# Fast form of the last convolution: even, odd and difference products of half width for every sample

## The chip, the cores and the metric

The kernel runs on one core of one Trainium2 chip. The metric is the device time of one execution in microseconds; the median of three runs of the kernel before is 755.43 us (754.4 to 756.1).

## The reference, cut to what matters

```python
def _layer(x, style, w, b, mw, mb, typ):
    s = style @ mw.T + mb                       # modulation, one vector per sample
    weight = SCALE * w * s[:, None, :, None]
    demod = lax.rsqrt(jnp.sum(weight * weight, axis=(2, 3)) + EPS)
    weight = weight * demod[:, :, None, None]
    if typ == 'same':         out = vmap(_conv_same)(x, weight) + b[None, :, None]
    elif typ == 'upsample':   out = _blur(vmap(_conv_up)(x, ...) + b[None, :, None], 2.0 * blur_k, (1, 1))
    elif typ == 'downsample': out = vmap(_conv_down)(_blur(x, blur_k, (2, 2)), weight) + b[None, :, None]
    return out
out = x
for i, typ in enumerate(('same', 'upsample', 'same', 'downsample')):
    out = _layer(out, style, weights[i], biases[i], mod_w[i], mod_b[i], typ)
return x + out                                  # x: (128, 64, 1024) float32
```

Each sample goes through four short convolutions whose weights are its own. Nothing nonlinear lies between them, so for one sample the four layers and the added x are one linear convolution (apart from two columns at each end, which are computed separately).

## The kernel before, in words

The samples are taken in 32 **groups** of four (g is the group, i the sample in it, b = 4g + i), and in 64 pairs (n) for loads, splits and stores.

For each sample the kernel first **composes** the four layers into one filter of five taps, 128 x 128 each: inputs and outputs hold even positions in partitions 0 to 63 and odd ones in 64 to 127, so a sample is 128 x 512 and the filter steps over columns. Composing is done for a whole group at once in seven **units** (g, u): u 0 and 1 make `Q2f`, u 2 and 3 make `Gf`, u 4, 5 and 6 make the taps `Wf`. A unit is 2 to 14 matmuls of 256 columns into one of four PSUM banks `pg`; then VectorE (`full`) scales the bank into `Q2f`, `Gf` or `Wf`, ScalarE (`high`) rounds it to a high part, and GpSimd (`low`, POOL in the profile) or, for the taps, VectorE (`w_low`) subtracts to get the low part. A group has 56 matmuls in its units: 10 in u 0 and 1, 24 in u 2 and 3, 22 in u 4 to 6. The lower and upper halves of the taps' other columns are filled by DMAs within SBUF (`cross`, on SP's queue).

The **convolution** of a sample (`conv`) is 5 taps x 3 products (high x high, high x low, low x high; `split_mm`) of 512 columns into `po[b % 2]`: 15 matmuls. Its x is loaded (`load`), rounded on ScalarE (`x_high`, 128 x 1032 for a pair) and its remainder taken on VectorE (`x_low`). ScalarE's `t_out` scales `po`, adds the bias term and writes `T`; GpSimd's `finish` copies the four end columns from `EP` into `T`; SP stores the pair (`store`). The end columns of 32 samples at a time come from `edge`, four steps of small matmuls on TensorE and chains of small operations on VectorE.

The order is written by hand. `SLOTS` says which units stand ahead of which sample: units 4 to 6 of the next group at i = 0, units 0 and 1 of the group after that at i = 1, unit 2 at i = 2 and unit 3 at i = 3. Every engine runs its own list in order and waits on semaphores.

## Time and profile before

| | |
|---|---|
| median of 3 runs | 755.43 us (754.4 to 756.1) |
| span of the profiled execution, first to last instruction | 755.1 us |
| TensorE busy | 711.5 us (94%), 3858 matmuls |
| VectorE, ScalarE, GpSimd busy | 342.5, 299.5, 281.6 us |
| mean granted TensorE clock | 0.982 of 2.4 GHz |

Matmul records overlap, since matmuls are pipelined: what one costs is read as the distance between the starts of two that follow one another. A row's own duration runs to the modelled end of its last column. For the other engines, durations are those of single instructions, and the next one starts some 0.09 us before the record of the one ahead of it ends. Idle time ahead of an instruction is in brackets, with what ended it.

### The profile page before, as it was taken

The numbers are of one execution on the slowest core, as the hardware profiler recorded it, in microseconds if no ns is written. First come the engines' busy times: TensorE is split into PE (matmuls) and PEld (weight loads), VectorE is DVE, ScalarE is ACT, GpSimd is POOL, SyncE is SP. The second block draws the span as 40 slices with busy tenths as digits, with TensorE's granted clock in tenths as the row PEclk, the third lists the DMA queues.
The fourth block names the chain that finished last, engine by engine and source line by source line (L and its number), as shares of the span: only waits on it lengthen the run. The fifth ranks groups of instructions, "written<-read, shape, count | busy, mean of one in ns | idle before, by whom it ended". The sixth has DMA issues, their size and how long they took to land.

```text
span 755.1 us, 10500 instructions
## 1 busy us (share of the span) xinstructions
PE 711.5 (94%) x3858; PEld 622.0 (82%) x3858; DVE 342.5 (45%) x551; ACT 299.5 (40%) x437; POOL 281.6 (37%) x456
## 2 busy tenths in 40 slices
PE   5668999998999999998999999999899999999997
PEld 4557888887888888887888888888788888888886
DVE  5968434435544333445335443453454443334430
ACT  3322444343434344434243444443334444443432
POOL 2431443442333443333443434434334434443310
PEclk9979999999999999999999999999999999999999
DMA  7043267764367767655756666677445777666572
GB/s 253 1 118 64 84 147 175 175 147 118 99 162 175 157 145 166 154 138 115 175 120 155 151 152 148 150 175 175 107 108 137 174 175 170 148 150 164 157 177 83
DMA packets 112162, 108.46 MB, mean 144 GB/s; under 512 B 4528, under 2 KB 78640, under 8 KB 112112
## 3 DMA queue, kind: packets, MB, share of 16 engines
q1 hardware_dynamic: 111456, 106.22, 58.6%
q10 hardware_dynamic: 656, 1.57, 0.6%
q8 instruction: 31, 0.51, 0.3%
q14 instruction: 19, 0.16, 0.1%
HBM read 36.47 MB, written 33.55 MB: 93 GB/s over the span
## 4 chain that ended last, share of the span: by engine, by line
PE 77%; DVE 10%; issue 6%; POOL 3%; ACT 2%; DMA 1%; POOLq 0%; ACTq 0%; DVEq 0%
PE po L159 16%; PE po L161 16%; PE po L160 16%; PE pg L159 7%; PE pg L161 6%; PE pg L160 6%; PE pg L164 3%; PE pg L165 3%; POOL Q2l L520 2%; DVE xl L595 1%; DVE Wf L617 1%; DVE Q2f L606 1%; POOL Q2h L168 1%; ACT Q2h L418 1%; ACT W L428 1%
## 5 line engine op out<-in xcount | busy, mean ns | idle before, releaser
L159 PE MATMUL po<-xh,W 128*128 128x512 f32 x640 | 254.5, 398 | 0.0
L160 PE MATMUL po<-xl,W 128*128 128x512 f32 x640 | 253.4, 396 | 0.0
L161 PE MATMUL po<-xh,W 128*128 128x512 f32 x640 | 253.4, 396 | 0.0
L595 DVE TENSOR_TENSOR xl<-X,xh 128x1032 fp32r<-128x1032 f32 x64 | 81.8, 1277 | 201.3 <-ACT xh L396 201.1
L403 ACT ACTIVATE T<-po,cv,DD 128x512 f32<-128x512 f32 x128 | 99.7, 779 | 169.2 <-PE po L161 167.7
L161 PEld LDWEIGHTS po<-xh,W 128*128 128x128 f32 x640 | 125.2, 196 | 24.5
L159 PEld LDWEIGHTS po<-xh,W 128*128 128x128 f32 x640 | 125.8, 197 | 20.6 <-issue 0.2
L160 PEld LDWEIGHTS po<-xl,W 128*128 128x128 f32 x640 | 125.6, 196 | 20.1
L520 POOL TENSOR_TENSOR Q2l<-Q2f,Q2h 128x512 fp32r<-128x512 f32 x31 | 40.0, 1290 | 228.3 <-ACT Q2h L418 228.3
L428 ACT CAST W<-Wf 128x512 fp32r<-128x512 f32 x64 | 46.6, 728 | 119.3 <-DVE Wf L617 93.0
L613 DVE TENSOR_TENSOR Gf<-pg,D10c 128x512 f32<-128x512 f32 x64 | 44.0, 689 | 103.8 <-PE pg L165 103.6
L528 POOL TENSOR_TENSOR Gl<-Gf,Gh 128x512 fp32r<-128x512 f32 x31 | 40.0, 1291 | 121.1 <-ACT Gh L423 121.1
L423 ACT CAST Gh<-Gf 128x512 fp32r<-128x512 f32 x64 | 39.6, 620 | 113.6 <-DVE Gf L613 113.6
L159 PE MATMUL pg<-Q2h,B1h 128*128 128x256 f32 x192 | 59.2, 309 | 19.6 <-POOL Q2h L168 15.7
L396 ACT CAST xh<-X 128x1032 fp32r<-128x1032 f32 x64 | 66.7, 1042 | 0.0
L159 PEld LDWEIGHTS pg<-Q2h,B1h 128*128 128x128 f32 x192 | 38.7, 202 | 33.2 <-issue 28.9
L159 PE MATMUL pg<-Gh,Ch 128*128 128x256 f32 x192 | 56.8, 296 | 1.3 <-DVE Gl L754 1.3
L630 DVE TENSOR_TENSOR W<-Wf,W 128x512 fp32r<-128x512 f32 x64 | 52.3, 817 | 11.0 <-ACT W L428 11.0
L161 PE MATMUL pg<-Q2h,B1l 128*128 128x256 f32 x192 | 56.9, 296 | 0.0
L160 PE MATMUL pg<-Q2l,B1h 128*128 128x256 f32 x192 | 56.8, 296 | 0.0
L160 PE MATMUL pg<-Gl,Ch 128*128 128x256 f32 x192 | 54.8, 285 | 0.0
L161 PE MATMUL pg<-Gh,Cl 128*128 128x256 f32 x192 | 54.8, 285 | 0.0
(154 smaller groups left out, 998.2 us busy)
## 6 DMA issues: line engine op xcount, KB each, us to landing
X<-in_xin SPq DMA_DIRECT2D x64, 516.0 KB, 5.3
out<-T SPq DMA_DIRECT2D x64, 512.0 KB, 3.1
W<-W SPq DMA_DIRECT2D x96, 256.0 KB, 6.6
W<-W SPq DMA_DIRECT2D x32, 384.0 KB, 7.6
E<-in_ed ACTq DMA_DIRECT2D x1, 768.0 KB, 8.5
XE<-in_xe SPq DMA_DIRECT2D x1, 576.0 KB, 11.1
Gf<-in_mwt SPq DMA_DIRECT2D x1, 256.0 KB, 3.2
A2f<-in_a ACTq DMA_DIRECT2D x1, 256.0 KB, 6.3
```

Source lines behind the costliest of these rows:

```text
L159: eng.matmul(o, wh_, rh, start=first, stop=False)
L160: eng.matmul(o, wh_, rl, start=False, stop=False)
L161: return eng.matmul(o, wl_, rh, start=False, stop=last)
L396: act.copy(xh[:, n % XH], X[:, n % XR]).then_inc(s_xh, 1)
L403: act.activation(T[:, n % TR, b % Q], po[b % 2][:, :], ACT.Identity, bias=cv[:, b:b + 1], scale=DD[:, 3, b:b + 1]).then_inc(s_t, 1)
L423: act.copy(Gh[:, :, v], Gf[:, :, v]).then_inc(s_gh, 1)
L428: act.copy(W[:, g % 2, v, 0, :, 0].rearrange("p v a m -> p a v m"), Wf[:, :, v]).then_inc(s_wh, 1)
L520: pool.tensor_tensor(Q2l[:], Q2f[:, :, 0:2], r32(Q2h[:, :, 0:2]), ALU.subtract).then_inc(s_q2l, 1)
L528: pool.tensor_tensor(Gl[:, :, 0:2], Gf[:, :, 0:2], r32(Gh[:, :, 0:2]), ALU.subtract).then_inc(s_gl, 1)
L595: tt(xl[:, n % XH], X[:, n % XR], r32(xh[:, n % XH]), ALU.subtract).then_inc(s_xl, 1)
L613: m = tt(cols(Gf[:, :, 2 * u - 4:2 * u - 2]), cols(bank(src, 2)), bc2(gs(D10c, g), 2), ALU.mult)
L630: tt(w[1], Wf[:, :, v], r32(w[0]), ALU.subtract).then_inc(s_wl, 1)
```

## The change

**The convolution in three products.** A sample is now held as 2 x 256 columns (even columns, odd columns, `H = 256`) and a third set, their difference (odd minus the next even, `columns(n)` on GpSimd). With the taps W0 to W4, `conv_even` multiplies the even columns by W0, W2, W4 into `pa` (which lies in the bank `ps`), `conv_odd` the odd ones by W1, W3 into `pb[b % 2]`, and `conv_diff` the differences by C1 = W0 - W1, C3 = W2 - W3 and W4 on top of `pb`. Each tap is 3 matmuls of 256 columns: 24 per sample in place of 15 of 512. W, xh, xl and X grow by the new taps and columns.

**The results.** ScalarE's `t_out` becomes `a_out` (pa, scaled and with bias, into `AB`) and `b_out` (pb, scaled, into `AB`). The even columns are their sum, taken on GpSimd (`even_out`); the odd ones are `pb` after `conv_diff`, scaled, plus the shifted first part, on VectorE (`odd_out`). `conv_diff(b - 1)` stands between `conv_even(b)` and `conv_odd(b)`, and waits until `b_out(b - 1)` has read `pb`.

**The taps.** VectorE makes the differences (`w_diff`, two per group); ScalarE rounds and VectorE subtracts in three parts in place of two, `w_high` and `w_low` (3 taps, 4 taps, and two taps of 64 partitions in `M`). `cross` has six DMAs in place of four, 1664 KB per group in place of 1152 KB.

**Other.** `finish` is gone: the end columns go out once, in an output of their own (`oute`), and are put in place on the host. The edge steps stand at i = 3 of every second group on TensorE and at i = 2 of the group after it on VectorE; before, those of the first 32 samples all stood in group 0. X has 3 buffers in place of 4, xh and xl 2 in place of 3, T 2 in place of 3. Units move: none at i = 1; 2 and 3 together at i = 2; 0 and 1, now of the group three ahead, at i = 3; and units 2 and 3 of group 1 are composed before the first sample. In the diff, the last three loops over b are those of ScalarE, GpSimd and VectorE.

```diff
-PROLOGUE = [(0, 0), (0, 1), (0, 2), (0, 3), (1, 0), (1, 1), (0, 4), (0, 5), (0, 6)]
...
-SLOTS = [[(1, 4), (1, 5), (1, 6)], [(2, 0), (2, 1)], [(2, 2)], [(2, 3)]]
+PROLOGUE = [(0, 0), (0, 1), (0, 2), (0, 3), (1, 0), (1, 1), (0, 4), (0, 5), (0, 6), (1, 2), (1, 3)]
...
+SLOTS = [[(1, 4), (1, 5), (1, 6)], [], [(2, 2), (2, 3)], [(3, 0), (3, 1)]]
...
+            def taps(b, o, e, js, onto=False):
+                g, i = divmod(b, NG)
+                n, q = divmod(b, Q)
+                for k, (j, start, stop) in enumerate(js):
+                    w = [W[:, g % 2, j - C1, t, i // 2].rearrange("p r (o b) -> p (r o) b", b=2)[:, :, i % 2]
+                         for t in range(2)]
+                    m = split_mm(pe, o, w[0], w[1], xh[:, n % XH, q, e, k:k + H], xl[:, n % XH, q, e, k:k + H], start, stop, onto)
+                return m
...
+            def conv_even(b):
                 g, i = divmod(b, NG)
                 n, q = divmod(b, Q)
                 if i == 0:
-                    pe.wait_ge(s_wh, 2 * g + 2)
-                    pe.wait_ge(s_wl, 2 * g + 2)
-                    pe.wait_ge(s_w[g % 2], 2 * 16 * ND * (g // 2 + 1))
+                    pe.wait_ge(s_wh, 3 * g + 2)
+                    pe.wait_ge(s_wl, 3 * g + 2)
+                    pe.wait_ge(s_w[g % 2], 16 * NX * (g // 2 + 1))
                 if q == 0:
                     pe.wait_ge(s_xh, n + 1)
                     pe.wait_ge(s_xl, n + 1)
+                if b:
+                    pe.wait_ge(s_ae, b)
+                taps(b, pa, 0, ((W0, True, False), (W2, False, False), (W4, False, True))).then_inc(s_a, 1)
+
+            def conv_odd(b):
                 if b >= 2:
-                    pe.wait_ge(s_t, b - 1)
-                for j in range(5):
-                    w = [W[:, g % 2, j, t, i // 2].rearrange("p r (o b) -> p (r o) b", b=2)[:, :, i % 2] for t in range(2)]
-                    m = split_mm(pe, po[b % 2][:, :], w[0], w[1], xh[:, n % XH, q, j:j + L2], xl[:, n % XH, q, j:j + L2],
-                                 j == 0, j == 4)
-                m.then_inc(s_o, 1)
+                    pe.wait_ge(s_yo, b - 1)
+                taps(b, pb[b % 2][:, 0:H], 1, ((W1, True, False), (W3, False, True))).then_inc(s_b, 1)
+
+            def conv_diff(b):
+                pe.wait_ge(s_be, b + 1)
+                taps(b, pb[b % 2][:, 0:H], 2, ((C1, False, False), (C3, False, False), (W4, False, True)),
+                     True).then_inc(s_p, 1)
...
             for b in range(B):
+                g, i = divmod(b, NG)
                 for x in units_of(b):
                     unit(*x)
-                conv(b)
-                if divmod(b, NG) in edge_at:
-                    edge(*edge_at[divmod(b, NG)])
+                conv_even(b)
+                if b:
+                    conv_diff(b - 1)
+                conv_odd(b)
+                if i == 3 and g % 2 == 0:
+                    edge(*divmod(g // 2, 4))
...
             def x_high(n):
                 act.wait_ge(s_x[n % XR], 16 * (n // XR + 1))
+                act.wait_ge(s_s, n + 1)
                 if n >= XH:
-                    act.wait_ge(s_o, Q * (n - XH + 1))
+                    act.wait_ge(s_p, Q * (n - XH + 1))
                 act.copy(xh[:, n % XH], X[:, n % XR]).then_inc(s_xh, 1)
...
                 g, i = divmod(b, NG)
-                if b == 1:
+                if b:
+                    b_out(b - 1)
+                else:
                     act.wait_ge(s_sc, SC_CV)
-                if b:
-                    t_out(b - 1)
-                if b % Q == 0 and b // Q + 2 < NQ:
-                    x_high(b // Q + 2)
+                n = (b + 1) // Q
+                if b % Q == 1 and XH <= n < NQ:
+                    x_high(n)
+                if i == 1 and g + 3 < NGR:
+                    q3_high(g + 3)
+                if i == 0:
+                    a_out(b)
                 for x in units_of(b):
-                    if x[1] != 5:
+                    if x[1] == 4:
+                        for k in range(3):
+                            w_high(x[0], k)
+                    elif x[1] < 4:
                         high(*x)
-                if i == 3 and g + 3 < NGR:
-                    q3_high(g + 3)
-            t_out(B - 1)
+                if i:
+                    a_out(b)
...
+                if b:
+                    even_out(b - 1)
+                n = b // Q + 1
+                if b % Q == 0 and XH <= n < NQ:
+                    columns(n)
+                if i == 0 and g + 3 < NGR:
+                    q3_full(g + 3)
                 for x in units_of(b):
                     if x[1] < 4:
                         low(*x)
-                if i == 2 and g + 3 < NGR:
-                    q3_full(g + 3)
-                if i == 3 and g + 3 < NGR:
+                if i == 1 and g + 3 < NGR:
                     q3_low(g + 3)
-                if b % Q == 1 and b > Q:
-                    finish(b // Q - 1)
-            finish(NQ - 1)
+                if i == 3 and g + 2 < NGR:
+                    identity(g + 2)
...
-                    c, k = edge_at[g, i]
+                    if x[1] == 4:
+                        w_diff(x[0], 0)
+                    elif x[1] == 6:
+                        w_diff(x[0], 1)
+                if b:
+                    odd_out(b - 1)
+                n = (b + 1) // Q
+                if b % Q == 1 and XH <= n < NQ:
+                    x_low(n)
+                for x in units_of(b):
+                    if x[1] == 4:
+                        for k in range(3):
+                            w_low(x[0], k)
+                if i == 2 and g % 2 == 1:
+                    c, k = divmod(g // 2, 4)
                     edge(c, k)
```

On ScalarE, at i = 0 of a group (`AB<-ps` is a_out, `AB<-pb` is b_out, `M` holds the two taps of 64 partitions), before:

```order
L428 CAST W<-Wf 128x2x2x128
L428 CAST W<-Wf 128x2x3x128
L403 ACTIVATE T<-po0,cv,DD 128x512
L418 CAST Q2h<-Q2f 128x2x256
L418 CAST Q2h<-Q2f 128x2x128
```

and of the change, from i = 0 to a_out of i = 1:

```order
L447 ACTIVATE AB<-pb1,DD 128x256 [waits b]
L442 ACTIVATE AB<-ps,cv,DD 128x256 [waits yo,ye,a]
L473 CAST W<-Wf 128x2x3x128 [waits p,cd]
L473 CAST W<-Wf 128x2x4x128 [waits p,cd]
L477 CAST M<-Wf 64x2x2x128 [waits w1,cd]
L447 ACTIVATE AB<-pb0,DD 128x256 [waits b]
L435 CAST xh<-X 128x1548 [waits p,s,x0]
L453 CAST Q3h<-Q3f 128x512 [waits c,q3f]
L442 ACTIVATE AB<-ps,cv,DD 128x256 [waits yo,ye,a]
```

The three roundings of the taps now stand between a_out of sample 0 and b_out of sample 0. On GpSimd, the same stretch (from the low parts of units 0 and 1 at i = 3 on), before:

```order
L520 TENSOR_TENSOR Q2l<-Q2f,Q2h 128x512 [waits q2h]
L168 TENSOR_TENSOR Q2h<-Q2f,Q2h 64x2x128 [waits q2l,q2h]
L546 COPY T<-EP 128x2x2 [waits ed,t,q2l]
L547 COPY T<-EP 128x2x2
L528 TENSOR_TENSOR Gl<-Gf,Gh 128x2x256 [waits gh]
```

and of the change:

```order
L582 TENSOR_TENSOR Q2l<-Q2f,Q2h 128x512 [waits q2h]
L180 TENSOR_TENSOR Q2h<-Q2f,Q2h 64x2x128 [waits q2l,q2h]
L601 TENSOR_TENSOR ID<-EYE,inv3 128x256 [waits ce,q2l]
L618 TENSOR_TENSOR T<-AB 128x256 [waits be,ae]
L609 TENSOR_TENSOR X<-X 128x2x257 [waits x2]
L569 TENSOR_TENSOR Q3f<-q3s,D32 128x256 [waits q3l,q3h]
L569 TENSOR_TENSOR Q3f<-q3s,D32 128x256
L618 TENSOR_TENSOR T<-AB 128x256 [waits st0,be,ae]
```

even_out (`T<-AB`) and the difference columns (`X<-X`) have come in between. On VectorE, from x_low at i = 3 to the low parts of the taps at i = 0, of the change:

```order
L674 TENSOR_TENSOR xl<-X,xh 128x1548 [waits xh]
L698 TENSOR_TENSOR Wf<-pg,S 128x2x256 [waits wh,c]
L708 TENSOR_TENSOR Wf<-Wf 128x2x256 [waits ce]
L698 TENSOR_TENSOR Wf<-pg,S 128x2x256 [waits wh,c]
L702 TENSOR_TENSOR Wf<-Wf,ID 64x2x128 [waits id,ch]
L698 TENSOR_TENSOR Wf<-pg,S 128x2x128 [waits wh,c]
L711 TENSOR_TENSOR Wf<-Wf 128x2x2x128 [waits ce]
L729 SCALAR_TENSOR_TENSOR T<-pb,DD,AB 128x256 [waits p,ae]
L716 TENSOR_TENSOR W<-Wf,W 128x2x3x128 [waits wh]
L716 TENSOR_TENSOR W<-Wf,W 128x2x4x128 [waits wh]
L720 TENSOR_TENSOR M<-Wf,M 64x2x2x128 [waits w1,wh]
```

Before, the same stretch there was x_low, the three `Wf<-pg` with the `Wf<-Wf,ID` between them, and two low parts; the two differences (`Wf<-Wf` alone), odd_out (`T<-pb,DD,AB`) and the low part in `M` are new.

## Rows read from the trace of the kernel before

**Rows 1.** Timeline, TensorE: start us, duration us, engine, line, operation, tiles, shape.

```profile
432.50 0.40 PE L161 MATMUL po<-xh,W 128*128 128x512 f32 x1
432.73 0.27 PE L159 MATMUL pg<-Q2h,B1h 128*128 128x256 f32 x1
432.84 0.28 PE L160 MATMUL pg<-Q2l,B1h 128*128 128x256 f32 x1
```

**Rows 2.** Timeline, TensorE: the same place of two groups of samples, one after the other.

```profile
427.50 0.36 PE L159 MATMUL pg<-Q2h,B1h 128*128 128x256 f32 x1
...
448.44 0.36 PE L159 MATMUL pg<-Q2h,B1h 128*128 128x256 f32 x1
```

**Rows 3.** Timeline, TensorE with its weight loads (PEld), from composing to a sample.

```profile
308.62 0.19 PEld L165 LDWEIGHTS pg<-Q3h,A2l 128*128 128x128 f32 x1
...
308.74 0.20 PEld L159 LDWEIGHTS po<-xh,W 128*128 128x128 f32 x1
...
308.86 0.40 PE L159 MATMUL po<-xh,W 128*128 128x512 f32 x1
```

**Rows 4.** Groups of instructions by shape: count | busy us, mean ns | idle before, releaser.

```profile
L403 ACT ACTIVATE T<-po,cv,DD 128x512 f32<-128x512 f32 x128 | 99.7, 779 | 169.2 <-PE po L161 167.7
...
L396 ACT CAST xh<-X 128x1032 fp32r<-128x1032 f32 x64 | 66.7, 1042 | 0.0
L159 PE MATMUL pg<-Q2h,B1h 128*128 128x256 f32 x192 | 59.2, 309 | 19.6 <-POOL Q2h L168 15.7 <-DVE Q2h L168 3.0
...
L520 POOL TENSOR_TENSOR Q2l<-Q2f,Q2h 128x512 fp32r<-128x512 f32 x31 | 40.0, 1290 | 228.3 <-ACT Q2h L418 228.3
...
L630 DVE TENSOR_TENSOR W<-Wf,W 128x768 fp32r<-128x768 f32 x32 | 30.7, 959 | 10.3 <-ACT W L428 10.3
L428 ACT CAST W<-Wf 128x768 fp32r<-128x768 f32 x32 | 26.7, 835 | 26.3 <-DVE Wf L623 26.3
...
L512 POOL TENSOR_TENSOR Q3l<-Q3f,Q3h 128x256 fp32r<-128x256 f32 x31 | 23.2, 750 | 6.3 <-ACT Q3h L410 4.1
...
L539 POOL TENSOR_TENSOR ID<-EYE,inv 128x256 f32<-128x256 f32 x32 | 20.0, 624 | 7.6 <-DVE inv L760 7.6
...
L608 DVE TENSOR_TENSOR Q2f<-pg,D 128x256 f32<-128x256 f32 x32 | 13.3, 415 | 0.0
```

**Rows 5.** Timeline, GpSimd (POOL) beside VectorE (DVE), before the first sample.

```profile
37.54 1.65 POOL L507 TENSOR_TENSOR Q3f<-q3s,D 128x256 f32<-128x256 f32 x2
38.02 0.69 DVE L630 TENSOR_TENSOR W<-Wf,W 128x512 fp32r<-128x512 f32 x1 [0.68 <-ACT W L428]
...
41.87 1.23 DVE L595 TENSOR_TENSOR xl<-X,xh 128x1032 fp32r<-128x1032 f32 x1
...
42.52 1.17 POOL L512 TENSOR_TENSOR Q3l<-Q3f,Q3h 128x256 fp32r<-128x256 f32 x1 [3.33 <-ACT Q3h L410]
```

**Rows 6.** Timeline, the same two engines later, in the main loop.

```profile
180.16 1.35 DVE L595 TENSOR_TENSOR xl<-X,xh 128x1032 fp32r<-128x1032 f32 x1 [2.28 <-ACT xh L396]
180.48 1.07 POOL L546 COPY T<-EP 128x4 f32<-128x4 f32 x1
...
181.50 0.18 POOL L547 COPY T<-EP 128x4 f32<-128x4 f32 x1
```

**Rows 7.** Stretch with taps in flight: busy us of each engine, clock, DMA share, GB/s.

```profile
318.00:323.00 5.00, 5.00 (x28) 4.42 (x27) 0.69 (x1) 2.24 (x4) 3.52 (x6) 1.00 1.23 196
```

**Rows 8.** Timeline: edge step 0 on TensorE, edge step 1 on VectorE (first and last row).

```profile
53.76 1.30 PE L326 MATMUL pe<-b1s,E 128*128 128x224 f32 x6
...
62.32 0.39 DVE L646 TENSOR_TENSOR AA<-pe,S 128x224 f32<-128x224 f32 x1 [1.49 <-PE pe L330]
...
65.98 1.05 DVE L658 SCALAR_TENSOR_TENSOR U<-AA,S 64x352 f32<-64x352 f32 x2
```

**Rows 9.** Timeline, TensorE: first matmul of unit 2 in group 0, of unit 4 in group 1.

```profile
71.97 0.36 PE L159 MATMUL pg<-Q2h,B1h 128*128 128x256 f32 x1 [3.00 <-POOL Q2h L168]
...
80.59 0.38 PE L159 MATMUL pg<-Gh,Ch 128*128 128x256 f32 x1
```

More of the change, by code:

```diff
@@ L370, in _ @@
             pe.wait_ge(s_cl, 1)
-            for x in PROLOGUE[6:9]:
+            for x in PROLOGUE[6:]:
                 unit(*x)
@@ L446, in _ @@
             act.wait_ge(s_in["cw"], 16)
-            act.copy(Ch[:], Cf[:]).then_inc(s_k0, 1)
+            act.copy(Ch[:], Cf).then_inc(s_k0, 1)
             q3_high(0)
@@ L469, in _ @@
             high(1, 1)
-            high(0, 4)
-            high(0, 6)
+            for k in range(3):
+                w_high(0, k)
+            high(1, 2)
+            high(1, 3)
             x_high(1)
@@ L495, in _ @@
             for d in range(2):
-                pool.memset(r32(W[lo, d, 0, :, :, 1]), 0.0)
+                pool.memset(r32(W[lo, d, W0 - C1, :, :, 1]), 0.0)
+            pool.memset(Wf[:, :, ZB], 0.0)
+            for r in range(XR - 1):
+                pool.memset(X[:, r, :, 2, XW - 1:XW], 0.0)
             for t in (ZE, Y, U, HH):
@@ L560, in _ @@
             low(1, 1)
+            low(1, 2)
+            low(1, 3)
             q3_full(2)
             q3_low(2)
+            identity(1)
             for b in range(B):
                 g, i = divmod(b, NG)
-                if i == 0 and g + 1 < NGR:
-                    identity(g + 1)
+                if b:
[5 more added lines that the diff above has]
+                    q3_full(g + 3)
                 for x in units_of(b):
@@ L767, in _ @@
             full(0, 4)
-            w_low(0, 0)
+            w_diff(0, 0)
             full(0, 5)
             full(0, 6)
-            w_low(0, 1)
+            w_diff(0, 1)
+            for k in range(3):
+                w_low(0, k)
             x_low(0)
@@ L783, in _ @@
             reached(dve.tensor_copy(cv[hi], cv[lo]))
+            link(dve.memset(AB[:, :, 0, H:H + 1], 0.0))
+            full(1, 2)
+            full(1, 3)
             x_low(1)
@@ L789, in _ @@
                 g, i = divmod(b, NG)
-                if b % Q == 0 and b // Q + 2 < NQ:
-                    x_low(b // Q + 2)
                 for x in units_of(b):
                     full(*x)
-                if (x := units_of(b)) and x[0][1] == 4:
-                    w_low(x[0][0], 0)
-                    w_low(x[0][0], 1)
-                if (g, i) in edge_at:
-                    c, k = edge_at[g, i]
+                    if x[1] == 4:
[9 more added lines that the diff above has]
+                    if x[1] == 4:
+                        for k in range(3):
+                            w_low(x[0], k)
+                if i == 2 and g % 2 == 1:
+                    c, k = divmod(g // 2, 4)
                     edge(c, k)
@@ L801, in _ @@
                         edge_in(c + 1)
+            odd_out(B - 1)
 def layouts(x, cond_512, w, bia, mw, mb):
```

229 lines of the change are left out of this document (142 added, 87 removed).

## The prediction

> **What bounds the kernel now.** I read the timeline of TensorE first. It is busy 94% of the span at a granted clock of 0.982, and a group of four samples repeats every 448.44 - 427.50 = 20.94 us [rows 2]. In it a matmul of 512 columns follows the last after 0.233 us, and one of 256 columns after 0.11 to 0.12 us; I use 0.1195, the mean over a whole unit [rows 1]. 60 x 0.2333 + 56 x 0.1195 = 20.7 us, so a group is TensorE alone, but for 0.2 us ahead of unit 2. The groups by shape then give the prices of the other engines [rows 4], and in them the other waits of TensorE: 15.7 us for GpSimd's low part ahead of unit 2. Last I looked at places where GpSimd and VectorE run beside each other [rows 5, 6], since the change gives both more to do.
>
> **The matmuls.** A sample goes from 15 x 0.2333 = 3.50 us to 24 x 0.1195 = 2.87 us; a group, with its 56 composing matmuls unchanged, to 152 x 0.1195 = 18.16 us. That holds if a matmul of 256 columns with taps as weights costs what one with composing weights does. The taps are read with a step of two elements, the composing weights without one. At the seam between the two the load of a tap starts at 308.74 and its matmul at 308.86, 0.12 us after the load's start, though its own record is 0.20 us [rows 3]. So a tap's load fits into the 0.12 us; I take 0.1195 and keep +0.01 as a bound, by which its record is longer than that of the composing weights ahead of it, 0.19. TensorE: Matmul & The Clock Gate of the Trainium skill (Back-to-back issue gap) gives 81 ns for 128 columns and 131 ns for 512 in a stream of load and matmul pairs. By that a half-width matmul costs far more than half. Rows 1 say 0.233 and 0.12, a little over half, and I go by them.
>
> **Work added on the other engines, per group.** ScalarE: a_out and b_out, 8 x 256 columns from PSUM. The nearest row is t_out, 512 columns in 0.779; x_high and w_high give 0.8 ns a column [rows 4], so 0.57 each (bounds 0.40 and 0.78). x_high grows to 1548 columns, 1.46 us. w_high is 0.84 + 1.04 + 0.62 where it was 0.62 + 0.84. VectorE: odd_out 4 x 0.42 (a 256-column read of PSUM [rows 4]), w_diff 2 x 0.67, w_low 0.96 + 1.23 + 0.67 (was 1.63), x_low 1.79 each (1.23 now, 1.08 ns a column more). GpSimd: even_out 4 x 0.62, columns 2 x 1.17 (0.62 for 256 columns of plain float32, bounds 1.17 and 1.29); finish goes.
>
> **GpSimd and VectorE hold each other up.** x_low runs from 41.87 to 43.10; GpSimd's subtraction started at 42.52 takes 1.17 us in place of 0.75 [rows 4]. Earlier two GpSimd products of 0.61 each take 1.65 with a w_low in between [rows 5]. A copy of 4 elements beside x_low takes 1.07, the next one, alone, 0.18, and x_low itself 1.35 in place of 1.23 [rows 6]. So operations with two SBUF inputs on the two engines go one after the other; each holds the way for its record less 0.15 us, and when both have something ready they alternate, as the 1.65 shows. VectorE's reads of PSUM (full, odd_out) don't take part. SBUF — State Buffer of the Trainium skill (Who interferes with whom) states this as an exclusive lock for the whole instruction, and the trace agrees. Before, the two hardly meet. Per group they now want, in records: VectorE 3.6 (x_low) + 1.3 + 2.9 + 0.4 = 8.2 us, and GpSimd 2.5 + 2.3 + 1.2 (q3_full) + 1.5 (q3_low) + 2.8 and 2.0 (low parts) + 0.6 (identity) = 12.9 us. 21.1 us less 0.15 for each of 24 is 17.5 us of the 18.2 that TensorE needs: nearly full, so they will queue.
>
> **The walk through one group**, t = 0 at the start of unit 4. TensorE wants: units 4 to 6 until 2.63, even(0) 3.70, diff of the last sample 4.78, odd(0) 5.50, even(1) 6.57, then diff(0), which waits for b_out(0). On the shared way: x_low until 1.54, low part of unit 1 until 2.13, w_diff 0 until 2.85, identity 3.31, even_out 3.89, the identity added to the tap 4.16, columns 5.18, w_diff 1 until 5.70 (record 5.85). ScalarE waits with the second w_high for it: 5.9 to 6.93, the third to 7.46, and only then b_out(0), 7.37 to 7.94. TensorE starts diff(0) at 8.05 in place of 6.57: 1.48 us of waiting, and everything behind it moves by as much. The other waits are met: a_out(0) ends at 4.5 for 5.50; the next x_low at 12.2 for even(2) at 12.7 (close); b_out(1) and b_out(2) have 1.1 us of matmuls as cover and need 0.8; a_out(3) and the x_low at i = 3 end 1 us before even(0) of the next group wants them, behind 2.63 us of units. The taps: last w_low at 9.6, six DMAs of 1.70 MB, at the 196 GB/s of such a stretch [rows 7] 8.7 us, done by 19; wanted at 22.3. A group is 18.16 + 1.48 = 19.64 us, and with no blocking (w_diff 1 done at 5.1) the wait would be 0.73.
>
> **Edges.** TensorE's part (0.95 us a step, 1.30 less the overlap of 0.35 [rows 8]) is the same, but the three steps that stood in the first group's later samples fall behind t = 80.6. On VectorE step 1 is a chain of 4.2 us (62.32 to 66.5 [rows 8]), step 2 some 3.4, step 0 1.2, step 3 with its input 2.0. They now stand at i = 2, between odd_out(1) and the full of unit 0. Step 1 pushes x_low past its slack (about 1.0 us of wait for even(0)) and w_diff with it (1.2 more at diff(0)); step 2 about 1.3 together, step 3 0.4, step 0 0.2: 4 x 4.1 = 16 us.
>
> **The start.** Unit 4 of group 1 starts at 80.59 [rows 9]. In front of it go three edge steps (2.9 us) and the 3.0 us wait of the first unit 2 [rows 9], composing 24 matmuls moves into an idle stretch, and the first four samples are shorter (2.5). Against it: unit 4 of the first group now waits for full, high and low of units 2 and 3, behind the whole chain on VectorE (about +5), and each queue is longer. I take 77, bounds 74 to 82.
>
> **The sum**, against the profiled 755.1 us (median 755.4, the same within its spread): groups 1 to 30, 30 x (19.64 - 20.94) = -39; group 31, 14.0 to 11.5 = -2.5; units 0 and 1 missing one group earlier, -1.2; start -3.6; the waits ahead of unit 2 after the start (15.7 [rows 4] less that 3.0) -12.7; edges on VectorE +16, on TensorE 3 x 0.95 = +2.9; in the last groups no units cover x_low, which ends 4.6 us into a pair's 2.87 us: 3 x 1.8 = +5.4; the end, with b_out between the last odd and diff, +1.4. Together -33, that is 722 us.
>
> **Rivals.**
> *The blocking costs little* (they meet less than I think, or alternate in a better order): wait 0.73 and edges 8 us: 722 - 22 - 8 = 692. For it: 17.5 of 18.2 is an average. Against: the chain up to w_diff 1 has GpSimd's backlog of i = 3 in it.
> *GpSimd comes first, slower than before.* At the end of i = 3 the low part of unit 0 (1.29 us [rows 4]) and x_low become ready within 1.2 us of each other. If GpSimd wins, x_low ends 1.14 later, even(0) waits 0.3 and w_diff 1, hence diff(0), 1.14 more: 30 x 1.4 = +43, 765 us. It decides from 1.1 us per group on.
> *Loads of taps bound the half matmuls.* 96 a group, of which the waits hide about 25: with +0.01 us 21 us more, 743; no gain is left from +0.016 on (a matmul every 0.135).
> *Half-width matmuls cost 0.75 of a full one*, the ratio by the pair rule named above: 24 x 0.175 = 4.2 us a sample, over 830 us. Rows 1 speak against it.
> *The taps' DMAs land late*, the change moving 1.45 times the bytes: from 3 us later on, some 2 us a group, 780.
>
> **How the numbers follow.** Forecast 0.55, little blocking 0.17, GpSimd first 0.13, loads of taps 0.08, late DMAs 0.05, half-width cost 0.02. Within 0.2%, which is about what a measurement can tell from no change, the same. Faster: forecast, little blocking, half of the loads and part of the spread, 0.80; same 0.03; slower 0.17. The range goes from little blocking to GpSimd first, 690 to 765.
>
> **What would show it.** Matmuls of the taps every 0.12 us; TensorE's longest wait at the first matmul of diff(0), released by b_out, 1 to 2 us in each group; x_low, w_diff or columns with records longer than alone; a group of 19 to 20.5 us. It is wrong if even(0) waits for x_low in plain groups, if a_out is what ends waits, or if matmuls of taps stand over 0.125 apart.

## The result

The changed kernel takes 763.45 us (median of 4 runs, 760.45 to 764.93) against 755.76 us before (754.4 to 756.75): a ratio of 1.0095, interval 1.007 to 1.0121. It is slower by 1%, where the prediction said faster by 4%. The profiled run has a span of 762.0 us against 755.1. These are the head of its page and the rows of the busy shares and the granted clock (40 slices).

```profile
span 762.0 us, 13801 instructions
PE 655.3 (86%) x5010; PEld 641.4 (84%) x5010; DVE 581.9 (76%) x776; ACT 380.0 (50%) x597; POOL 550.7 (72%) x524
...
PE   5568999889798999989799899989989899988976
...
PEclk9959999999899999989999999989999999999999
```

TensorE is busy for 655.3 us where it was for 711.5, and stands idle for more than it saved. What it waits for is in the groups of instructions by shape (count | busy us, mean ns | idle before, releaser). They answer to [rows 4].

```profile
L171 PE MATMUL pb<-xh,W 128*128 128x256 f32 x640 | 189.3, 296 | 57.6 <-ACT AB L447 57.6
L171 PE MATMUL ps<-xh,W 128*128 128x256 f32 x384 | 112.0, 292 | 16.6 <-DVE xl L674 15.0 <-issue 1.6
L674 DVE TENSOR_TENSOR xl<-X,xh 128x1548 fp32r<-128x1548 f32 x64 | 119.7, 1871 | 2.1 <-ACT xh L435 2.1
...
L447 ACT ACTIVATE AB<-pb,DD 128x256 f32<-128x256 f32 x128 | 60.6, 474 | 61.3 <-PE pb L173 60.5
...
L473 ACT CAST W<-Wf 128x1024 fp32r<-128x1024 f32 x32 | 33.5, 1046 | 19.4 <-DVE Wf L711 19.4
...
L582 POOL TENSOR_TENSOR Q2l<-Q2f,Q2h 128x512 fp32r<-128x512 f32 x31 | 55.1, 1779 | 46.4 <-ACT Q2h L461 45.8
```

b_out (L447) ends 57.6 us of waits ahead of diff, and x_low (L674) another 15.0 ahead of even. ScalarE itself waits 19.4 us for w_diff 1 (L711) ahead of the second rounding of the taps (L473), which b_out stands behind. The durations of a_out, b_out, odd_out, x_high and x_low are the forecast ones within 0.1 us. The operations of GpSimd and VectorE with two SBUF inputs have longer records, since what they wait for each other is inside them: GpSimd's low part (L582) 1.78 us in place of the 1.29 of [rows 4], its columns 1.41 for 1.17, and w_diff 1.05 and 0.97 for 0.67.

**A plain group.** This is what I call a group without edge work on VectorE just ahead of it (it stands right behind an edge step of TensorE). Its timeline on TensorE: unit 4, the seam between even(1) and diff(0), and unit 4 of the next group. These answer to [rows 2].

```profile
301.69 0.41 PE L171 MATMUL pg<-Gh,Ch 128*128 128x256 f32 x1
...
308.28 0.28 PE L173 MATMUL ps<-xh,W 128*128 128x256 f32 x1
309.83 0.39 PE L171 MATMUL pb<-xh,W 128*128 128x256 f32 x1 [1.27 <-ACT AB L447]
...
321.62 0.28 PE L171 MATMUL pg<-Gh,Ch 128*128 128x256 f32 x1
```

The group lasts 19.93 us (forecast 19.64) and diff(0) starts 8.14 after unit 4 (forecast 8.05). A matmul of the taps follows the last after 0.12 us. This part went as forecast.

**The groups behind an edge chain.** Every second group comes after the edge chain of VectorE at sample 2 of the group before. Here are the chain of step 1 on VectorE and what stands behind it, and then TensorE at even(0) of the next group.

```profile
317.48 0.38 DVE L746 TENSOR_TENSOR AA<-pe,S 128x224 f32<-128x224 f32 x1
...
318.16 0.75 DVE L751 TENSOR_SCALAR Y<-AA,BB 64x224 f32<-64x224 f32 x1
318.83 0.89 DVE L752 TENSOR_SCALAR Y<-AA,BB 64x192 f32<-64x192 f32 x1
319.73 0.71 DVE L751 TENSOR_SCALAR Y<-AA,BB 64x224 f32<-64x224 f32 x1
320.37 0.33 DVE L752 TENSOR_SCALAR Y<-AA,BB 64x192 f32<-64x192 f32 x1
...
322.51 1.05 DVE L758 SCALAR_TENSOR_TENSOR U<-AA,S 64x352 f32<-64x352 f32 x2
323.59 0.69 DVE L685 TENSOR_TENSOR Q2f<-pg,D 128x512 f32<-128x512 f32 x1
...
324.92 1.76 DVE L674 TENSOR_TENSOR xl<-X,xh 128x1548 fp32r<-128x1548 f32 x1
```

```profile
321.62 0.28 PE L171 MATMUL pg<-Gh,Ch 128*128 128x256 f32 x1
...
326.94 0.55 PE L171 MATMUL ps<-xh,W 128*128 128x256 f32 x1 [2.09 <-DVE xl L674]
...
333.05 0.31 PE L172 MATMUL ps<-xl,W 128*128 128x256 f32 x1
```

The chain runs from 317.48 to 323.56, 6.1 us. Before it took 4.7: the last row of [rows 8] holds two operations and ends at 67.03. x_low ends at 326.7, which is 5.1 us after unit 4 began; even(0) wanted it after 2.6. TensorE waits 2.09 us, and then runs at its lower clock: up to 333.05 its matmuls stand 0.213 apart. The stretches of TensorE (busy us, granted clock, DMA share, GB/s) show the same.

```profile
326.00:328.00 2.00, 1.06 (x5) 0.57 0.15 13
328.00:330.00 2.00, 2.00 (x11) 0.50 0.73 251
...
332.00:334.00 2.00, 1.84 (x11) 0.72 0.21 75
```

0.50 is the 1.2 GHz of the two levels, and TensorE had been busy but for short waits until the one of 2.09. Some 29 matmuls from 326.94 to 333.05 lose (0.213 - 0.12) each, 2.7 us, so that the wait of 2.09 costs 4.8. This group lasts 26.03 us (321.62 to 347.65), with a mean granted clock of 0.87, where the plain one has 1.00 (busy us of PE, PEld, DVE, ACT and POOL, then the clock, DMA share and GB/s):

```profile
301.69:321.62 19.93, 18.66 (x154) 18.46 (x153) 16.60 (x24) 9.72 (x14) 14.95 (x15) 1.00 0.72 172
321.62:347.65 26.03, 23.13 (x160) 22.14 (x159) 20.75 (x27) 13.33 (x22) 20.52 (x18) 0.87 0.62 163
```

The chains of the other steps are shorter, and the groups behind them are late too. One behind step 0 (from 278.87) and one behind step 3 (from 235.99), with the busy us of PE, the clock, DMA share and GB/s; then ScalarE and GpSimd in the second of them:

```profile
278.87:301.69 22.82, 20.97 (x161) 0.93 0.67 185
235.99:258.89 22.90, 19.54 (x160) 1.00 0.69 178
```

```profile
243.89 1.04 ACT L473 CAST W<-Wf 128x1024 fp32r<-128x1024 f32 x1 [2.00 <-DVE Wf L711]
```

```profile
236.63 2.82 POOL L582 TENSOR_TENSOR Q2l<-Q2f,Q2h 128x512 fp32r<-128x512 f32 x1 [1.94 <-ACT Q2h L461]
```

Here x_low is in time, but the full parts of units 0 and 1 stood behind the chain, so GpSimd's low part starts late, meets x_low and takes 2.82 us in place of 1.29. The identity and w_diff 1 are late behind it, ScalarE waits 2.00 us for w_diff 1, and TensorE 3.36 us for b_out. The clock stays at 1.00 after that wait. In the group from 278.87 the wait for b_out is 1.85, and the clock reads 0.50 from 289 to 291. So the length of a wait doesn't tell whether the clock falls; what does is not shown here.

From the first to the last of 28 groups, in the same columns, the changed kernel takes:

```profile
78.88:702.58 623.70, 557.90 (x4342) 0.96 0.67 172
```

That is 22.27 us a group. The same 28 groups of the kernel before, from 80.59 to 698.98, with most of the edge steps in them too, take 22.09 each. I read the starts of all of them: in the changed kernel plain groups are 19.9 to 20.5, those with an edge chain ahead 22.8 to 27.5.

### The profile page after: what moved, and what is told of

Same layout as the page of the kernel before. It is cut to its first block, busy times and chain, and to the rows that moved or that the text cites. A ratio compares the mean times of both kernels' runs of the same rounds, so it can differ in the third digit from the quotient of the medians.

```text
span 762.0 us, 13801 instructions
## 1 busy us (share of the span) xinstructions
PE 655.3 (86%) x5010; PEld 641.4 (84%) x5010; DVE 581.9 (76%) x776; ACT 380.0 (50%) x597; POOL 550.7 (72%) x524
## 4 chain that ended last, share of the span: by engine, by line
PE 55%; DVE 20%; issue 11%; POOL 7%; ACT 6%; DMA 0%; ACTq 0%; DVEq 0%; POOLq 0%
PE pb L171 8%; PE pb L173 7%; PE pb L172 7%; PE pg L171 5%; PE pg L172 5%; PE pg L173 5%; POOL Q2l L582 4%; DVE Wf L698 4%; PE ps L171 3%; DVE Wf L711 3%; PE ps L172 3%; PE ps L173 3%; PE pg L176 2%; PE pg L177 2%; ACT M L477 2%
## 5 line engine op out<-in xcount | busy, mean ns | idle before, releaser
L171 PE MATMUL pb<-xh,W 128*128 128x256 f32 x640 | 189.3, 296 | 57.6 <-ACT AB L447 57.6
L172 PE MATMUL pb<-xl,W 128*128 128x256 f32 x640 | 185.7, 290 | 0.0
L173 PE MATMUL pb<-xh,W 128*128 128x256 f32 x640 | 185.4, 290 | 0.0
L171 PEld LDWEIGHTS pb<-xh,W 128*128 128x128 f32 x640 | 129.8, 203 | 63.9 <-ACT AB L447 63.9
L618 POOL TENSOR_TENSOR T<-AB 128x256 f32<-128x256 f32 x128 | 92.6, 723 | 84.8 <-issue 54.7
L442 ACT ACTIVATE AB<-ps,cv,DD 128x256 f32<-128x256 f32 x128 | 72.2, 564 | 119.9 <-PE ps L173 119.9
L173 PEld LDWEIGHTS pb<-xh,W 128*128 128x128 f32 x640 | 130.1, 203 | 0.0
L172 PEld LDWEIGHTS pb<-xl,W 128*128 128x128 f32 x640 | 129.7, 203 | 0.0
L171 PE MATMUL ps<-xh,W 128*128 128x256 f32 x384 | 112.0, 292 | 16.6 <-DVE xl L674 15.0
L674 DVE TENSOR_TENSOR xl<-X,xh 128x1548 fp32r<-128x1548 f32 x64 | 119.7, 1871 | 2.1 <-ACT xh L435 2.1
L172 PE MATMUL ps<-xl,W 128*128 128x256 f32 x384 | 110.8, 289 | 0.0
L173 PE MATMUL ps<-xh,W 128*128 128x256 f32 x384 | 110.5, 288 | 0.0
L435 ACT CAST xh<-X 128x1548 fp32r<-128x1548 f32 x64 | 94.5, 1477 | 0.0
L171 PEld LDWEIGHTS ps<-xh,W 128*128 128x128 f32 x384 | 77.4, 201 | 18.6 <-issue 18.6
L447 ACT ACTIVATE AB<-pb,DD 128x256 f32<-128x256 f32 x128 | 60.6, 474 | 61.3 <-PE pb L173 60.5
L582 POOL TENSOR_TENSOR Q2l<-Q2f,Q2h 128x512 fp32r<-128x512 f32 x31 | 55.1, 1779 | 46.4 <-ACT Q2h L461 45.8
L473 ACT CAST W<-Wf 128x768 fp32r<-128x768 f32 x64 | 59.4, 943 | 41.0 <-DVE Wf L711 19.4
L173 PEld LDWEIGHTS ps<-xh,W 128*128 128x128 f32 x384 | 77.2, 201 | 0.0
```

The source lines that it names most:

```text
L171: eng.matmul(o, wh_, rh, start=first, stop=False, skip_group_check=onto)
L172: eng.matmul(o, wh_, rl, start=False, stop=False, skip_group_check=onto)
L173: return eng.matmul(o, wl_, rh, start=False, stop=last, skip_group_check=onto)
L435: act.copy(xh[:, n % XH], X[:, n % XR]).then_inc(s_xh, 1)
L442: act.activation(AB[:, b % AR, 0, 0:H], pa, ACT.Identity, bias=cv[:, b:b + 1], scale=DD[:, 3, b:b + 1]).then_inc(s_ae, 1)
L447: act.mul(AB[:, b % AR, 1, 0:H], pb[b % 2][:, 0:H], DD[:, 3, b:b + 1]).then_inc(s_be, 1)
```

## The experiments

All stand against the same kernel before (755.7 to 756.0). A kernel's clock loss below is (1 - mean granted clock) x span: at 0.5 the same work takes twice as long, so for a busy engine it is the time that the lower clock cost, and an upper bound where TensorE is idle at it.

| run | us | ratio, interval | wait for b_out | for x_low ahead of even | clock loss |
|---|---|---|---|---|---|
| changed kernel | 763.45 | 1.0095 [1.007, 1.0121] | 57.6 | 15.0 | 35.1 |
| no edges | 705.96 | 0.9347 [0.932, 0.9375] | 49.1 | 3.5 | 14.1 |
| b_out first | 745.57 | 0.9856 [0.9803, 0.9908] | 0.6 | 39.3 + 10.7 | 26.0 |
| GpSimd's columns for 1 of 257 | 744.43 | 0.985 [0.9826, 0.9874] | 53.7 | 11.4 | 23.0 |
| b_out first, no edges | 687.78 | 0.910 [0.9076, 0.9124] | 0.6 | 5.2 + 30.6 | 11.0 |
| edges on TensorE only | 719.37 | 0.9526 [0.9498, 0.9554] | 45.9 | 3.0 | 12.2 |
| chain spread | 757.79 | 1.0022 [1.0004, 1.0041] | 58.0 | 2.8 | 33.2 |
| chain with PSUM operands | 759.89 | 1.005 [1.0019, 1.0081] | 58.4 | 14.1 | 34.2 |
| chain spread, PSUM operands | 728.37 | 0.9631 [0.9584, 0.9677] | 51.0 | 3.0 | 19.7 |
| chain spread, b_out first | 738.6 | 0.9771 [0.9719, 0.9823] | 0.6 | 19.7 + 24.5 | 27.4 |
| the same, taps later | 750.58 | 0.9932 [0.9907, 0.9958] | 0.6 | 0 + 5.0 | 29.2 |
| spread, PSUM, b_out first | 718.75 | 0.9511 [0.9459, 0.9563] | 0.6 | 13.7 + 30.0 | 17.9 |
| the same, taps later, a_out first | 696.82 | 0.921 [0.9165, 0.9254] | 7.8 | 0 + 8.3 | 13.2 |

A second number in the fifth column is a wait at the same matmul for which the trace names no releaser ("issue"). Waits for a_out ahead of even are not in the table: 5.2 us with the chain spread, 8.7 with b_out first on it, 54.9 with the taps later.

**Are the edges what is missing?** The edge steps are left out on both engines:

```diff
-                if i == 3 and g % 2 == 0:
-                    edge(*divmod(g // 2, 4))
...
-                if i == 2 and g % 2 == 1:
-                    c, k = divmod(g // 2, 4)
-                    edge(c, k)
-                    if k == 3 and c + 1 < B // EC:
-                        edge_in(c + 1)
```

> The edge steps are left out on TensorE and VectorE (the end columns of the output are zeros); all else is the changed kernel. Theory A: what the forecast missed is the edge chains on VectorE, which push x_low and w_diff, and the half clock that follows the longer waits. In the trace of the changed kernel 28 groups from 78.88 to 702.58 us take 623.7 us; 28 x 20.0 (the plain groups) and 14 x 0.95 (the edge steps on TensorE) are 573.3, so 50 us go with the chains, and all groups should now take 20.0: about 763 - 15 - 52 = 696 us. Rival B: the even groups are longer because the shared way of GpSimd and VectorE is full, with or without edges: only TensorE's 15 us go, 748 us.

705.96 us. All groups are now alike, 20.14 us, with one wait of 1.6 us each, for b_out. The edges cost 57 us. The sum had 16 for VectorE's part; TensorE's 16 steps, 15 us at 0.95 each, stood in the kernel before as well, and only 2.9 of them are a term of it. Theory A was right on the kind and 10 us too low, 4 of them because it took groups of 20.0.

**What sets the wait for b_out?** b_out of sample 0 goes ahead of the second and third rounding of the taps on ScalarE:

```diff
                     if x[1] == 4:
-                        for k in range(3):
+                        w_high(x[0], 0)
+                        b_out(b)
+                        for k in (1, 2):
                             w_high(x[0], k)
```

> On ScalarE, b_out of sample 0 of a group stands ahead of the second and third rounding of the taps, behind the first; nothing else is changed. Theory A: TensorE's 57.6 us of waits for b_out at diff(0), and with them most of the half clock (some 20 us), go: 685 to 715 us. Rival B: the shared way is full, and the wait only moves, to x_low ahead of even(0) or to the taps' DMAs: 745 to 765 us.

745.57 us. The wait for b_out is gone in every group, but x_low now ends 39.3 us of waits, ahead of even. Rival B, at the edge of its range: the wait moved more than it went. A kernel with only this edit already beats the kernel before by 1.4%.

**Or do GpSimd's columns set it?** They are computed for 1 column of 257:

```diff
-                pool.tensor_tensor(x[:, :, 2, 0:XW - 1], x[:, :, 1, 0:XW - 1], x[:, :, 0, 1:XW], ALU.subtract).then_inc(s_s, 1)
+                pool.tensor_tensor(x[:, :, 2, 0:1], x[:, :, 1, 0:1], x[:, :, 0, 1:2], ALU.subtract).then_inc(s_s, 1)
```

> GpSimd's difference columns are computed for one column of 257 (the odd outputs are wrong); the operation, its place and its waits stay. Theory A, blocking: w_diff 1 no longer waits behind it and ends some 0.9 us earlier in each group, so diff(0) waits 0.9 us less: 763 - 30 = 733 us, and up to 15 less where the clock stays up, 715 to 735. Rival C, no blocking that matters: GpSimd is on no path to diff(0), 760 to 763 us.

744.43 us, between the two. The plain groups stay at 19.9 to 20.1 with their wait of 1.27, and the gain is in the groups behind an edge chain (those behind step 0: 21.1 in place of 22.8). So in a plain group it isn't w_diff 1, held up by GpSimd's columns, that makes b_out late, as the walk had it. In the changed kernel ScalarE around that place reads:

```profile
305.72 0.57 ACT L442 ACTIVATE AB<-ps,cv,DD 128x256 f32<-128x256 f32 x1 [4.31 <-PE ps L173]
306.86 1.79 ACT L473 CAST W<-Wf 128x768 fp32r<-128x768 f32 x2 [0.57 <-PE pb L173]
308.67 0.61 ACT L477 CAST M<-Wf 64x512 fp32r<-64x512 f32 x1
309.31 0.47 ACT L447 ACTIVATE AB<-pb,DD 128x256 f32<-128x256 f32 x1
```

The first rounding waits for the last matmul of diff of the group before (its taps' buffer comes free by it, in a ring of two), and from 306.86 on ScalarE is busy without a gap, 2.9 us, until b_out ends. That wait of ScalarE is the same with 1 column in 257: "PE pb L173" ends 17.9 us of its waits in 30 groups there, 19.1 in the changed kernel. A ring of three would show it from the other side; it needs 28 KB more in each partition and wasn't tried.

The walk was for a group without any edge work, and those stand in the run without edges. There ScalarE reads, in the group from 319.82:

```profile
324.86 0.84 ACT L471 CAST W<-Wf 128x768 fp32r<-128x768 f32 x1 [0.57 <-PE pb L173]
325.93 1.05 ACT L471 CAST W<-Wf 128x1024 fp32r<-128x1024 f32 x1 [0.23 <-DVE Wf L709]
```

So here w_diff 1 does end the last wait, at 6.1 us into the group where the walk had 5.85. But it sets only 0.23 us: one step earlier the first rounding, behind diff of the last sample, is nearly as late.

**Both together, without edges.**

> Both: no edge steps, and b_out of sample 0 ahead of the second and third rounding. Theory A: a group is TensorE alone, 152 x 0.1205 = 18.3 us, so 79 + 31 groups less the missing units + the end = 645 to 660 us. Rival B: GpSimd and VectorE, whose records in the changed kernel sum to 551 and 582 us, set a group of 19.5 us or more: 680 us and up.

687.78 us, which is what rival B wanted (680 and up), and 18 us under the run without edges alone. A wait of 1.0 us is left in each group, ahead of even(2). The timeline of VectorE there:

```profile
281.11 2.53 DVE L718 TENSOR_TENSOR W<-Wf,W 128x768 fp32r<-128x768 f32 x2
283.67 1.02 DVE L722 TENSOR_TENSOR M<-Wf,M 64x512 fp32r<-64x512 f32 x1
284.72 0.49 DVE L731 SCALAR_TENSOR_TENSOR T<-pb,DD,AB 128x256 f32<-128x256 f32 x1
285.12 1.87 DVE L676 TENSOR_TENSOR xl<-X,xh 128x1548 fp32r<-128x1548 f32 x1
```

and of TensorE:

```profile
287.09 0.36 PE L171 MATMUL ps<-xh,W 128*128 128x256 f32 x1 [1.02 <-issue]
```

x_low ends at 286.99 and even(2) starts at 287.09. It stands behind 3.6 us of low parts of the taps, which even(2) doesn't need.

**Which part of the edges: TensorE's or VectorE's?** A memset stands for each chain of VectorE:

```diff
             def edge(c, k):
                 cs = slice(c * EC, (c + 1) * EC)
                 dve.wait_ge(s_e, 4 * c + k + 1)
-                if k == 0:
...
+                dve.memset(EP[lo, c, 0:1], 0.0).then_inc(s_ed, 1)
```

> Leaves out VectorE's part of the edge values (one memset stands for each step's chain), so the edge output is not the reference's; TensorE's steps, 16 in all, stay. Theory A: TensorE's steps cost what their matmuls take, 16 x 0.95 = 15 us, over the 706 us without edges: 721 us (718 to 726); VectorE's block is then the other 42 us. Rival B: each step also costs a wait or a change of the clock: above 730.

719.37 us, theory A. TensorE's 16 steps cost 13 us over the 706, and VectorE's chains the other 44. The 28 groups between the same two matmuls as above take 577.4 us:

```profile
78.88:656.28 577.40, 535.36 (x4342) 1.00 0.73 186
```

That is 46.3 us less than the 623.7, for the same 4342 matmul records: 22.5 us of it TensorE was busy longer, which is the lower clock, and 23.8 us longer it stood idle, waiting. The table says the same: changed kernel less this run is 11.7 in waits for b_out, 12.0 in waits for x_low and 22.9 in the clock. Group by group, against this run, one behind the chain of step 0 or 3 is 1.7 us longer, one behind step 1 4.5 (the first 6.0) and one behind step 2 4.5 (the first 5.6).

**Is it that the chain stands in one block?** The same operations, but one link of the chain behind each sample, over seven samples of two groups:

```diff
-                if i == 2 and g % 2 == 1:
+                if i == 0 and g % 2 == 1:
                     c, k = divmod(g // 2, 4)
                     edge(c, k)
...
+                piece()
...
```

> The edge work of VectorE is the same, operation by operation, but no longer stands in one block at sample 2 of every second group: one operation (or independent pair) of the chain follows each sample, over seven samples of two groups. Theory A: what costs 57 us in all (run without edges, 706) is 16 us of TensorE's own steps plus the block: a chain of up to 6.1 us that holds x_low back, TensorE's waits for it and the lower clock behind the longest of them. Then 706 + 16 = 722 us, within 716 to 730, the groups all between 20.0 and 21.0, and the clock back at 0.98. Rival B: VectorE's sum of work is what counts, wherever it stands; then above 750.

757.79 us. Theory A fell and the time is rival B's: only 6 of 44 us are gained. The groups of VectorE's operations show why. First this run, then the run with PSUM operands that follows, for the same steps of the chain.

```profile
L674 DVE TENSOR_TENSOR xl<-X,xh 128x1548 fp32r<-128x1548 f32 x64 | 132.1, 2064 | 2.1 <-ACT xh L435 2.1
...
L770 DVE TENSOR_SCALAR Y<-AA,BB 64x224 f32<-64x224 f32 x8 | 8.3, 1035 | 0.1
...
L753 DVE TENSOR_TENSOR AA<-Y 128x416 f32<-128x416 f32 x4 | 6.2, 1545 | 0.0
```

```profile
L763 DVE SCALAR_TENSOR_TENSOR pe<-Y,pe 128x352 f32<-128x352 f32 x8 | 4.2, 523 | 0.1
L789 DVE SCALAR_TENSOR_TENSOR U<-pe,S 64x352 f32<-64x352 f32 x8 | 4.1, 517 | 0.1
L781 DVE TENSOR_SCALAR Y<-pe,BB 64x224 f32<-64x224 f32 x8 | 3.6, 446 | 0.1
```

Spread out, most of the small operations meet one of GpSimd: 416 columns take 1.55 us where they took 0.59 in the block, and 224 columns of a TENSOR_SCALAR 1.04 where they took 0.73. The block had been the cheaper place: there GpSimd runs out of work at 320.3 and waits until 325.0, and only the first half of the chain meets it.

**Operands in PSUM.** The chain's operations get an operand in TensorE's bank of the edges; three additions become four operations with a factor:

```diff
-                    link(tt(Y1[:, :, 0:13], Y[:, :, 1:14], Y[:, :, 0:13], ALU.add))
-                    link(tt(Y2[:, :, 0:12], Y1[:, :, 1:13], Y1[:, :, 0:12], ALU.add))
-                    link(tt(Y1[:, :, 0:11], Y2[:, :, 1:12], Y2[:, :, 0:11], ALU.add))
+                    P = pe_[:, 0:11 * EC].rearrange("p (b n) -> p b n", n=11)
+                    link(dve.tensor_scalar(P, Y[:, :, 0:11], 1.0, None, ALU.mult))
+                    for o, f in ((1, 3.0), (2, 3.0), (3, 1.0)):
+                        link(dve.scalar_tensor_tensor(out=P, in0=Y[:, :, o:o + 11], scalar=f, in1=P, op0=ALU.mult, op1=ALU.add))
```

In one block, as in the changed kernel:

> The changed kernel with VectorE's edge chain in the same block, but each of its operations now has an operand in TensorE's PSUM bank of the edges (the filter sums are four operations with a factor in place of three additions); only the input product keeps two SBUF inputs. Theory A: the operations cost what they do because GpSimd and VectorE wait for each other on two-input operations of SBUF: records of the chain fall to 0.3 to 0.5 each, the chain of step 1 from 6.1 to about 4.5 us, and of the 44 us that VectorE's part costs (763 - 719) a third goes: 745 to 755, since 4 us of block still hold x_low back. Rival B: the block's length hardly depends on the blocking, 760 or more.

759.89 us, rival B's value but for 0.1; the 3.6 us under the changed kernel are not clear of the noise, since the two intervals overlap. The chain of step 1 ends after 5.6 us in place of 6.1: its records are 0.4 to 0.55 and no longer held up, but there are more of them. A block of 5.6 us makes x_low as late as one of 6.1.

Spread and with PSUM operands:

> Both: operands in PSUM, and the operations spread over seven samples as in the run that spread them (757.8). Theory A: there each operation of 0.35 to 0.5 us had a record of 0.75 to 1.55 because it waited for GpSimd; with a PSUM operand it takes 0.3 to 0.5, fits between, and VectorE's part costs under 10 us: 722 to 732. Rival B: VectorE's order (x_low behind one more operation, x_low itself longer) is what costs, not the waiting for GpSimd: 748 and more.

728.37 us, theory A. Spreading alone gives 6 us, PSUM operands alone 4 at most, both give 35 of the 44. The cost has two parents: as a block the chain holds x_low up whatever its operands, and spread out it is held up by GpSimd unless it keeps off the way that they share.

**b_out first, on the spread chain.** With operands in SBUF:

> The spread chain, and b_out of sample 0 ahead of the second and third rounding of the taps on ScalarE. Without edges the second edit gave 706 - 688 = 18 us. Theory A: the two gains add, 722 - 18 = 704 us (698 to 712), with a wait of about 1.0 us left ahead of even of sample 2, which x_low ends. Rival B: the small operations of the chain now stand between the full parts and x_low and lengthen that wait, 720 and more.

and with operands in PSUM:

> As the run before this one, with b_out of sample 0 ahead of the second and third rounding of the taps. Without edges the edit was worth 18 us, with the block as well (763 to 746), with the spread chain 19. Theory A: 727 - 18 = 709 (704 to 715). Rival B: x_low, which is what ends waits once b_out doesn't, still has one operation more ahead of it in every sample: 720 and more.

738.6 us is rival B, though only since the kernel under it had missed its forecast: the edit itself is worth 19 us there, about what it is without edges (18). 718.75 is between the two: the edit is worth 10 us, and x_low ends the waits that are left.

**The taps behind x_low.** On top of the run with the chain spread, b_out first and operands in SBUF, the second and third rounding and low part move behind x_high and x_low of sample 1:

```diff
-                for x in units_of(b):
-                    if x[1] == 4:
-                        for k in range(3):
-                            w_low(x[0], k)
+                if i == 0 and g + 1 < NGR:
+                    w_low(g + 1, 0)
+                if i == 1 and g + 1 < NGR:
+                    for p in (1, 2):
+                        w_low(g + 1, p)
```

> As the run before this one, and besides the second and third rounding of the taps (ScalarE) and their low parts (VectorE, 1.63 and 1.02 us) stand behind x_high and x_low of sample 1, in place of in front of them. Theory A: in the run without edges the low parts are what held x_low back and so made the 1.0 us wait ahead of even of sample 2; it goes, and no other is late: 704 - 30 = 674 us (668 to 685), groups of 18.3 us. Rival B: the taps' six transfers, which now start some 2 us later, land behind the first even of the next group, and the wait stands there: 690 to 704 us. Rival C: another queue (full or low part of units 2 and 3) becomes late ahead of the units: 685 to 700.

750.58 us, worse than all three theories and 12 us over the run under it. The wait for x_low is gone, and one for a_out has come, 54.9 us, up to 3.1 at a time:

```profile
L171 PE MATMUL ps<-xh,W 128*128 128x256 f32 x384 | 116.7, 304 | 63.1 <-ACT AB L442 54.9 <-issue 5.0 <-DMA W<-M 3.0
```

I had looked for the next late one among the transfers and the low parts. It was ScalarE's queue:

```profile
308.01 1.21 ACT L466 CAST Gh<-Gf 128x512 fp32r<-128x512 f32 x2 [5.10 <-DVE Gf L697]
309.13 0.56 ACT L442 ACTIVATE AB<-ps,cv,DD 128x256 f32<-128x256 f32 x1
```

a_out of sample 2 (L442) stands behind the high parts of units 2 and 3, which wait 5.10 us for VectorE, now busy with low parts and a link of the chain; even(3) wanted a_out 3.1 us earlier. So a_out goes ahead of the high parts, and the chain gets its PSUM operands:

```diff
+                if i:
+                    a_out(b)
                 for x in units_of(b):
                     if x[1] == 4:
...
                         high(*x)
-                if i:
-                    a_out(b)
```

> As the run before this one, with the second and third rounding and low part of the taps behind x_high and x_low of sample 1, and on ScalarE a_out of samples 1 to 3 ahead of the high parts of the units of its sample. In the earlier try of the first edit (750.6) the waits of 2 to 3 us stood ahead of even, for a_out, which stood behind high parts that waited for VectorE. Theory A: with a_out ahead these waits go and the group is TensorE alone, 18.3 to 18.6: 682 to 692. Rival B: VectorE is behind by then and another of its results (x_low or the full part of unit 3) is waited for: 705 and more.

696.82 us, 5 over theory A's range, 7.9% under the kernel before and 8.7% under the changed one. Against 718.75 it is 22 us for the two moves together; a_out ahead of the high parts was not run by itself. The matmuls with the longest waits:

```profile
L171 PE MATMUL pb<-xh,W 128*128 128x256 f32 x640 | 186.1, 291 | 14.4 <-ACT AB L447 7.8 <-DVE T L734 6.0
L171 PE MATMUL ps<-xh,W 128*128 128x256 f32 x384 | 110.8, 289 | 11.3 <-issue 8.3 <-DMA W<-M 3.0
```

## Why the prediction was wrong

Its terms, in its order:

- **The matmuls.** Right: 0.12 us each, with taps as weights too. The loads of taps bound nothing, and the rival's price of 0.75 of a full matmul is refuted: it is 0.12 against 0.233.
- **Added work on the other engines.** Right within 0.1 us: a_out 0.56, b_out 0.47, odd_out 0.48, x_high 1.48, and x_low 1.87 with its waits in it. That GpSimd and VectorE hold each other up was right as well, and shows in the longer records of w_diff, columns and the low parts.
- **The walk.** The number was near: diff(0) starts 8.14 into a plain group and 8.35 into one without any edge work, against 8.05. Its cause was right in part, and luck helped. It left out that the first rounding waits for diff of the last sample, so ScalarE's four operations start at 5.0 to 5.2 and end b_out almost by themselves; w_diff 1 adds 0.23 us without edges and nothing in plain groups. So the wait of 0.73 without blocking, on which the rival of 692 stands, was not to be had. A group without edges lasts 20.14 in place of 19.64: 0.5 x 30 = 15 us.
- **The start.** 78.88 in place of 77: 2 us, within its bounds.
- **The edges on VectorE, +16 us.** This is the step that failed: they cost 44. The prediction said "Step 1 pushes x_low past its slack (about 1.0 us of wait for even(0)) and w_diff with it (1.2 more at diff(0))", 2.2 together, and 1.3 for step 2, 0.4 for step 3 and 0.2 for step 0. The groups behind them are longer by 4.5, 4.5, 1.7 and 1.7 us, the first ones by more. Three things were wrong:
  - *The length of the chain.* 4.2 us was read off [rows 8], whose last row holds two operations: it was 4.7, in a stretch in which GpSimd ran nothing. In the changed kernel it is 6.1, and the 1.4 more are its four TENSOR_SCALARs beside GpSimd.
  - *The path.* The full parts of units 0 and 1 stand behind the chain too, so GpSimd's low part comes late and falls on x_low, and w_diff 1 and b_out are late even behind the short chains of steps 0 and 3. Over 28 groups the chains add 23.8 us of waits; 16 had been forecast for all.
  - *The clock.* The delay was priced at TensorE's wait alone. The prediction says nothing of the clock, which takes 0 in its sum; it cost 22.5 of the 46.3 us of those groups, and its mean fell from 0.982 to 0.954. The trace of the kernel before had it to be read. There TensorE waits 2.70 us for GpSimd at 180.56, and then, busy all along:

```profile
182.00:184.00 2.00, 2.00 (x8) 0.50 0.70 255
```

The step is 28 of the 41.5 us between 722 and 763.45. The run with TensorE's edge steps only shows the rest: 719.4, where the sum less its 16 is 706. These 13.4 us are a little less than the 15 of the groups and the 2 of the start; which term gave back the difference is open.

Of the rivals, *GpSimd first* gave 765, nearly the time that was measured, by a mechanism that isn't there, so its number is luck: at the end of i = 3 ahead of the plain group x_low starts at 300.67 and takes its 1.76, and it is GpSimd's operation of 300.72 that takes 2.31 in place of 0.74. *Little blocking* (692) falls as well. The true case, edges that cost nearly three times as much, was none of them, and the side of slower had no rival on the edges at all. The sign of what would show it wrong was there in part: "if even(0) waits for x_low in plain groups" was looked for in the wrong groups.

"VectorE's reads of PSUM (full, odd_out) don't take part" in the blocking, the forecast held, and the runs with PSUM operands bear it out. It took only operations with two SBUF inputs to be blocked, though. The chain's TENSOR_SCALAR has one, and its rows at 318.16 to 319.73 are 0.7 to 0.9 beside GpSimd; the last one, at 320.37, has nothing beside it and takes 0.33. SBUF — State Buffer of the Trainium skill (Who interferes with whom), which the prediction cited for the lock, lists tensor_scalar among the operations that can take the shared pair, and states that one with at most one SBUF input outside those modes doesn't contend. The trace agrees with both: Y from AA (64x224) takes 1.04 us on average in the spread chain, Y from PSUM 0.45. The prediction used half of the section.
